# A graph layer on one core: each node search reads its own stretch of the loaded destinations, the load comes in two transfers, and the order test moves ahead of the first lists

## The chip, the cores and the metric

The kernel runs on one core of one Trainium2 chip. The metric is the device time of one execution in microseconds. Before the change it is 862.87 us, the median of 3 runs (862.81 to 863.2). The engines are TensorE (PE in the profile), VectorE (DVE), ScalarE (ACT), GpSimd (POOL) and SyncE (SP). SP, ACT and POOL issue transfers, and only POOL issues the indirect ones, which fetch from an address per partition.

## The reference

```python
def reference(x, src, dst, L0_gnn_W, L0_gnn_b):
    # x: 6250 nodes x 128; src, dst: 206250 edges, sorted by dst
    # (two random ends of 100000 edges, both ways, and one self edge per node)
    def _L0_gnn_ref(x, W, b, edge_index):
        src, dst = (edge_index[0], edge_index[1])
        x_i = x[dst]
        x_j = x[src]
        feat = jnp.concatenate([x_i, x_j - x_i], axis=-1)
        msg = feat @ W.T + b
        out = jax.ops.segment_max(msg, dst, num_segments=x.shape[0])
        return jnp.where(jnp.isfinite(out), out, 0.0)
    edge_index = jnp.stack([src, dst])
    h = jnp.maximum(_layernorm(x, axis=-1), 0.0)
    x = x + _L0_gnn_ref(h, L0_gnn_W, L0_gnn_b, edge_index)
    return x
```

Per node it is a maximum, over the node's incoming edges, of a row computed from the source node ("near"), plus a part of the node's own.

## The kernel before

**Tiling.** The 6250 nodes lie as 128 partitions by 49 columns; partition p owns nodes 49p to 49p+48. The edges are sorted by destination, so a partition's edges are one stretch of `dst` and `src`.

**Finding the edges (L925 to L976).** 512 samples of `dst`, one each `hop` = 403 edges, are compared with each partition's first node; a product on PE counts them (`count_ps`), and DVE turns the count into `begin_i`, the edge at which the partition's window begins. POOL then issues one indirect transfer (L713): every partition loads WIN = 2196 destinations. DVE casts them to f32 (L986), and `find` (L960) looks for the partition's 49 nodes and the next one, eight nodes per instruction, seven instructions, each over all 2196 columns. `find(0, 16)` and `begins(0)` give the start and the length of the list of the first 15 columns, the rest of `find` and `begins(1)` those of the other 34. Between them stand `statistics` and `scales`, which normalise x. When the starts are known, POOL issues one indirect transfer per column (L719, 15 and then 34), which loads the sources of 64 edges for each node.

**Lists (L1025), sort, words, compaction.** For each of the two parts (columns 0 to 14, columns 15 to 48) DVE masks the lists, sorts them by a network of 21 steps and packs those edges which the dense part below can't serve ("losers") into a list of 136, then 368, entries per partition.

**Two ways to the maximum.** Losers go through the chain: POOL gathers one row of `near_table` per partition and entry (L746, 503 gathers), and DVE takes a running maximum (`chain_step`, L1278). All others go through 196 dense rounds: ACT makes a one-hot matrix, PE multiplies (L869), DVE takes the maximum (L1334). At the end 49 final gathers on POOL (L725) fetch each node's chain result, and DVE joins both.

**What sets the order.** `schedule()` writes DVE's order after the first list by hand: a row of pieces with assumed costs (lists, three pieces named "check", 21 sorts, flags, words, moves, dense rounds, trees), between which it puts groups of 4 chain steps as soon as its assumed clock says that their rows have landed. The three "check" pieces are the order test: are the destinations sorted, and does every node occur? They read all of `dst` a second time, loaded by SP as `chk_i` (L434), 125 partitions by 1650, and write flags that are summed later. `then` and `settled` are a count of DVE's own finished instructions and a wait for it.

Queues: SP issues the samples, six chunks of x (L429; the fourth waits for `begin_ready`), the last rows of x, then waits for the window (`win_in`) and issues `chk_i` and x once more by rows. POOL issues the window, then waits for `starts_ready`.

Of the kernel before, what the change touches and what calls it, by code (L numbers as in the profile page):

```python
# [13 lines left out]
P = 128  # L14
F32 = mybir.dt.float32
# [19 lines left out]
SPAN = 1792  # L35

# [65 lines left out]
def schedule():  # L102
# [4 lines left out]
    pieces = [("lists", 11.0, 2.2), ("check", 1.1, 1.5), ("check", 1.9, 1.5), ("check", 1.9, 1.5)]  # L107
# [50 lines left out]
def edgeconv(nc, x, src, dst, W, b, out):  # L158
# [38 lines left out]
    with ExitStack() as ctx:  # L197
        def sb(name, shape, dt):
            return ctx.enter_context(nc.sbuf_tensor(name, shape, dt))

        def sem(name):
            return ctx.enter_context(nc.semaphore(name))
# [51 lines left out]
        begin_i = sb("begin_i", [P, 1], I32)  # L254
        pos = sb("pos", [P, 56], U32)
# [8 lines left out]
        flags = sb("flags", [P, 11], F32)  # L264
        flag_s = sb("flag_s", [P, 11], F32)
# [41 lines left out]
        def bank(i):  # L307
            return ps[:, i * 512:(i + 1) * 512]
# [7 lines left out]
        flag_ps = bank(7)[:, 0:11]  # L316
# [22 lines left out]
        win_in = sem("win_in")  # L339
# [82 lines left out]
        def _(sp):  # L422
            with nc.allow_non_contiguous_dma(reason="one edge in every hop"):
                smp_src = bass.AP(dst.tensor, dst.offset, [[4 * hop, P], [hop, 4]])
                sp.dma_start(smp_i[:, :], smp_src).then_inc(smp_in, 16)
            for c, (a, z) in enumerate(chunks):
                if c == 3:
                    sp.wait_ge(begin_ready, 1)
                sp.dma_start(x_nat[:, a:z, :], x_tiles[:, a:z, :]).then_inc(x_in[c], 16)  # L429
            sp.wait_ge(x_pad_set, 1)  # L430
            sp.dma_start(x_nat[0:rest, full, :], x[full * P:nodes, :]).then_inc(x_in[len(chunks)], 16)
            sp.wait_ge(win_in, 16)
# [263 lines left out]
        def _(pool):  # L696
# [5 lines left out]
            nc.gpsimd.memset(x_nat[:, full, :], 0.0).then_inc(x_pad_set, 1)  # L702
            nc.gpsimd.iota(iot_s, [[1, KS * 15]], base=1, channel_multiplier=0).then_inc(iota_set, 1)
# [3 lines left out]
            for q in range(1, len(opens)):  # L707
                if opens[q] > opens[q - 1]:
# [4 lines left out]
            nc.gpsimd.indirect_dma_start(win_i, None, dst[:, None],  # L713
                                         bass.IndirectOffsetOnAxis(begin_i[:, 0:1], 0)).then_inc(win_in, 16)
# [171 lines left out]
        def _(dve):  # L886
            own = [0]

            def then(ins):
                own[0] += 1  # L890
                ins.then_inc(dve_step, 1)

            def settled():
                dve.wait_ge(dve_step, own[0])
# [65 lines left out]
            def find(a, z):  # L960
                for c in range(a, z, 8):
                    then(V.max_index(pos[:, c:c + 8], tgt[:, c:c + 8], win))

            def begins(h):
# [3 lines left out]
                then(V.tensor_copy(start[:, at], pos[:, at]))  # L968
# [16 lines left out]
            dve.wait_ge(win_in, 16)  # L985
            then(V.tensor_copy(win, win_i))  # L986
# [3 lines left out]
            statistics(1)  # L990
            find(16, 32)
# [5 lines left out]
            then(V.tensor_tensor(flags[:, 0:1], win[:, WIN - 1:WIN], tgt[:, tiles:wide], ALU.is_lt))  # L997
            settled()
# [7 lines left out]
            def check():  # L1006

                dve.wait_ge(chk_in, 32)
                then(V.tensor_copy(chk[0:chk_p, :], chk_i[0:chk_p, :]))
                yield  # L1010
# [4 lines left out]
                yield  # L1015
# [3 lines left out]
                yield  # L1019
# [315 lines left out]

            lists(0)
# [9 lines left out]
            checks, flagging, wording, moving = check(), loser_flags(1), second_words(), compact(1)  # L1346
# [70 lines left out]
```

## Time and profile before

| | |
|---|---|
| median of 3 runs | 862.87 us |
| profiled execution, first to last instruction (the page gives no other time of it) | 862.0 us |
| DVE busy | 790.4 us, 92% |
| POOL busy | 619.0 us, 72% |
| PE busy | 544.8 us, 63% |
| ACT busy | 422.6 us, 49% |
| gathers L746 on POOL | 503, 516.1 us, mean 1026 ns |
| dense maxima L1334 on DVE | 196, 343.5 us |
| chain steps L1278 on DVE | 503, 176.8 us |

Busy time of POOL leaves out the 0.30 us that it takes between two gathers without waiting for anything; the profile puts it down as "issue". So a POOL that issues without a break looks 76% busy. Times below are from the start of the span.

### The profile page before, as it was taken

To read this page: it belongs to the slowest core of one execution; us is meant where nothing else is said; L and a number is where in the kernel's file an instruction comes from. 1 tells how busy PE (TensorE), PEld (TensorE's weight loads), DVE (VectorE), ACT (ScalarE), POOL (GpSimd) and SP (SyncE) were. 2 spreads that over 40 slices of the span, in tenths; PEclk is the share of its full clock that TensorE was granted. 3 is DMA by queue.
4 is the path that set the end of the run, shared out by engine and by line. 5 is a ranking of instruction groups with operands and counts; after the bars stand their busy time and mean duration, and the time that the engine had idled before them with its cause. 6 is when DMAs were issued, how large, how long until landed. Compare 5 with 4: busy or idle time off the path is not lost.

```text
span 862.0 us, 8032 instructions
## 1 busy us (share of the span) xinstructions
PE 544.8 (63%) x2442; PEld 263.8 (31%) x2442; DVE 790.4 (92%) x1283; ACT 422.6 (49%) x279; POOL 619.0 (72%) x631
## 2 busy tenths in 40 slices
PE   1565898000000677787766857788888888888871
PEld 1553466000000223232222323233333333333341
DVE  7989999989999899989989899899999998898897
ACT  3785314060147077656577569655565655742000
POOL 1577267788777777677777776777767777777774
PEclk9799899555555799988989988999999999999995
DMA  8951003232374766455655556556555666444347
GB/s 253 218 153 25 10 15 95 69 83 68 96 210 99 237 165 197 134 176 141 184 155 169 155 139 184 157 182 191 173 174 177 193 180 221 159 118 138 76 96 212
DMA packets 114693, 126.74 MB, mean 147 GB/s; under 512 B 19542, under 2 KB 96836, under 8 KB 114379
## 3 DMA queue, kind: packets, MB, share of 16 engines
q1 hardware_dynamic: 95090, 86.33, 33.0%
q0 software_dynamic: 19376, 38.94, 18.2%
q10 hardware_dynamic: 184, 0.96, 0.3%
q8 instruction: 19, 0.31, 0.1%
q14 instruction: 24, 0.20, 0.1%
HBM read 86.43 MB, written 40.57 MB: 147 GB/s over the span
## 4 chain that ended last, share of the span: by engine, by line
DVE 41%; POOL 19%; issue 19%; DMA 11%; PE 7%; ACT 1%; POOLq 0%; DVEq 0%; SPq 0%
POOL rows L746 14%; DMA rows<-near_table,idx 8%; DVE maxima L1278 8%; DVE acc L1334 8%; PE ps L869 7%; POOL hT L725 3%; DVE ohs L1240 3%; DVE sorts_mem L1068 2%; DVE sorts_mem L1067 2%; DVE hT L1287 2%; DVE ohs L1231 2%; POOL ohs L719 2%; DVE ohs L1229 1%; DVE rows L1240 1%; DMA ohs<-in_dst,begin_i 1%
## 5 line engine op out<-in xcount | busy, mean ns | idle before, releaser
L746 POOL DMA_INDIRECT rows<-near_table,idx x503 | 516.1, 1026 | 181.2 <-issue 132.8
L869 PE MATMUL ps<-ohs,near 128*128 128x481 fp8e3 x1404 | 319.0, 381 | 82.9 <-DVE acc L1334 76.3
L1334 DVE TENSOR_TENSOR acc<-ps,acc 128x1924 f32<-128x1924 f32 x196 | 343.5, 1779 | 29.3 <-PE ps L869 29.0
L607 ACT ACTIVATE ohs<-ohs,spike 128x6272 fp8e3<-128x6272 uint8 x36 | 197.9, 5513 | 72.0 <-DMA ohs<-winners 72.0
L869 PEld LDWEIGHTS ps<-ohs,near 128*128 128x128 bf16 x1404 | 134.3, 100 | 267.7 <-DVE acc L1334 90.2
L1278 DVE SCALAR_TENSOR_TENSOR maxima<-maxima,fresh,rows 128x128 f32<-128x128 f32 x503 | 176.8, 351 | 17.3 <-DMA rows<-near_table,idx 3.6
L602 ACT ACTIVATE hT<-k,off 128x1600 bf16<-128x1600 int16 (+6 forms) x49 | 65.9, 1392 | 154.8 <-DVE hT L1292 154.8
L869 PE MATMUL ps<-sorts_mem,near 128*128 128x481 fp8e3 x507 | 116.3, 385 | 28.1 <-DVE acc L1334 25.4
L607 ACT ACTIVATE sorts_mem<-sorts_mem,spike 128x6272 fp8e3<-128x6272 uint8 x13 | 71.7, 5515 | 35.9 <-DMA sorts_mem<-winners 35.9
L857 PE MATMUL ps<-flags,ones 128*128 128x11 f32 x2 | 0.6, 362 | 138.5 <-DVE spare L1312 138.5
L869 PEld LDWEIGHTS ps<-sorts_mem,near 128*128 128x128 bf16 x507 | 49.2, 101 | 94.9 <-DVE acc L1334 31.0
L719 POOL DMA_INDIRECT ohs<-src_pad,start_i x49 | 52.2, 1066 | 31.2 <-DVE start_i L975 16.9
L725 POOL DMA_INDIRECT hT<-running_max,end_row x49 | 47.0, 959 | 14.9 <-issue 14.3
L857 PEld LDWEIGHTS ps<-flags,ones 128*128 128x128 f32 x2 | 0.5, 310 | 138.6 <-issue 138.6
L589 ACT COPY base<-ps 128x512 f32<-128x512 f32 (+1 forms) x13 | 7.3, 562 | 40.7 <-PE ps L840 40.7
L1240 DVE COPY_PREDICATED ohs<-ohs 128x556 int32<-128x556 int32 (+9 forms) x40 | 26.2, 730 | 0.1
L840 PEld LDWEIGHTS ps<-wT,hT 128*128 128x128 f32 x98 | 23.5, 309 | 5.1 <-issue 3.7
L785 PE MATMUL ps<-ident,k 128*128 128x128 f32 x49 | 10.0, 335 | 23.3 <-ACT k L544 23.3
L811 PE MATMUL ps<-wT,hT 128*128 128x128 f32 x98 | 13.9, 285 | 15.8 <-ACT near L574 15.8
L840 PE MATMUL ps<-wT,hT 128*128 128x128 f32 x98 | 22.3, 373 | 0.0
L544 ACT ACTIVATE k<-acc,shift,rstd 128x128 f32<-128x128 f32 x49 | 20.1, 482 | 2.7 <-DVE shift L957 2.7
L614 ACT ACTIVATE ohs<-sorts_mem,j_bias 128x64 int32<-128x64 int16 x34 | 10.4, 403 | 22.2 <-DVE k L1075 22.2
(192 smaller groups left out, 472.6 us busy)
## 6 DMA issues: line engine op xcount, KB each, us to landing
running_max<-maxima SPq DMA_DIRECT2D x63, 512.0 KB, 3.6
ohs<-winners SPq DMA_DIRECT2D x36, 784.0 KB, 6.1
sorts_mem<-winners SPq DMA_DIRECT2D x13, 784.0 KB, 6.2
rows<-near_table,idx POOLq DMA_INDIRECT x503, 3.1
acc<-in_x SPq DMA_DIRECT2D x6, 512.0 KB, 8.0
near_table<-acc SPq DMA_DIRECT2D x12, 256.0 KB
base<-in_x SPq DMA_DIRECT2D x1, 2744.0 KB
out_x<-hT SPq DMA_DIRECT2D x12, 224.0 KB
```

The source lines that it names most:

```text
L544: last = nc.scalar.activation(xn[:, g % 2, j - spans[g][0], :], x_nat[:, j, :], ACT.Identity, bias=shift[:, j:j + 1], scale=rstd[:, j:j + 1])
L602: nc.scalar.activation(y[g % 2][:, t - a, 0:end - first, :], k2[:, first:end, :], ACT.Abs, bias=off[:, t:t + 1]).then_inc(y_made, 1)
L607: nc.scalar.activation(oh[t % OHS], oh_bytes[t % OHS], ACT.Abs_reciprocal_sqrt, bias=spike[:, 0:1], scale=float(SPIKE), saturate=False).th ...
L719: nc.gpsimd.indirect_dma_start(L[:, j, :], None, src_pad[:, None], bass.IndirectOffsetOnAxis(start_i[:, j:j + 1], 0)).then_inc(list_in[h], 16)
L725: nc.gpsimd.indirect_dma_start(rowsF[:, j, :], None, running_max[0:cap * P, :], bass.IndirectOffsetOnAxis(end_row[:, j:j + 1], 0)).then_in ...
L746: nc.gpsimd.indirect_dma_start(rows[:, n % (SLOTS * GATHERS), :], None, near_table[:, :], bass.IndirectOffsetOnAxis(idx[:, n:n + 1], 0)).t ...
L840: last = nc.tensor.matmul(bank(g % 3)[:, (j - a) * D:(j - a + 1) * D], hT[:, j:j + (P - 1) * tiles + 1:tiles], wT[:, 1, :], start=False, s ...
L869: last = nc.tensor.matmul(bank(4 * (n % 2) + c - UNITS[r][0])[:, 0:CHUNK], near[:, t, part, :], oh[t % OHS][:, at:at + CHUNK], start=part ...
L1067: then(V.tensor_tensor(two[:, :, 0:d, :], one[:, :, 0:d, :], one[:, :, d:2 * d, :], ALU.min))
L1240: then(V.copy_predicated(two[:, u:v], off_word[:, u + d:v + d], one[:, u:v]))
L1278: V.scalar_tensor_tensor(run_at(n + 1), run_at(n), fresh[:, n:n + 1], rows[:, n % (SLOTS * GATHERS), :], ALU.add, ALU.max).then_inc(chain, 1)
L1334: V.tensor_tensor(into, found[:, 0:z - a, 0:CHUNK], into, ALU.max).then_inc(max_done, 1)
```

## The change

- Partition 127's window is no longer computed: SP loads the last 1093 destinations into it right after the samples. The other 127 partitions load their window in two indirect transfers, columns 0 to 1026 (`win_in[0]`) and 1027 to 2195 (`win_in[1]`). The rest of partition 127's row is filled by a memset. `begin_i` is written straight from a clamp with per-partition bounds.
- `find` looks for the eight nodes of group k only in columns 236k-76 to 735+292k, cut to the window: 735, 867, 923, 979, 1035, 1091 and 856 columns, instead of seven times 2196. `look_i`, made on POOL, is added to the positions. Three new flags test that the stretches were wide enough.
- Two searches stand behind the cast of the near part; the far part is cast after `statistics(1)`.
- On SP the fourth chunk of x waits for the near part, and `chk_i` for the far part.
- The order test runs ahead of `lists(0)` in one piece; "check" is gone from the table, which changes where chain steps stand: 100 instead of 104 are done ahead of the sum of the flags, and 16 instead of 12 (504 places in all) are left behind the dense rounds.

```diff
 SPAN = 1792
+LAST_SPAN = 1093
+FAR_NODE = 1 << 16
+LOOK_FROM, LOOK_FROM_STEP = -76, 236
+LOOK_TO, LOOK_TO_STEP = 735, 292
+NEAR_SPAN = LOOK_TO + LOOK_TO_STEP
...
-    pieces = [("lists", 11.0, 2.2), ("check", 1.1, 1.5), ("check", 1.9, 1.5), ("check", 1.9, 1.5)]
+    pieces = [("lists", 11.0, 2.2)]
...
                 sp.dma_start(smp_i[:, :], smp_src).then_inc(smp_in, 16)
+            sp.dma_start(win_i[P - 1:P, 0:LAST_SPAN], dst[edges - LAST_SPAN:edges][None, :]).then_inc(last_in, 16)
             for c, (a, z) in enumerate(chunks):
                 if c == 3:
-                    sp.wait_ge(begin_ready, 1)
+                    sp.wait_ge(win_in[0], 16)
...
-            sp.wait_ge(win_in, 16)
+            sp.wait_ge(win_in[1], 16)
...
             nc.gpsimd.memset(x_nat[:, full, :], 0.0).then_inc(x_pad_set, 1)
+            nc.gpsimd.iota(look_i[:, :, :], [[LOOK_FROM_STEP, 7], [0, 8]], base=LOOK_FROM, channel_multiplier=0)
+            pool.drain()
+            nc.gpsimd.memset(look_i[:, 0, :], 0).then_inc(look_set, 1)
...
-            nc.gpsimd.indirect_dma_start(win_i, None, dst[:, None],
-                                         bass.IndirectOffsetOnAxis(begin_i[:, 0:1], 0)).then_inc(win_in, 16)
+            nc.gpsimd.indirect_dma_start(win_i[0:P - 1, 0:NEAR_SPAN], None, dst[:, None],
+                                         bass.IndirectOffsetOnAxis(begin_i[0:P - 1, 0:1], 0)).then_inc(win_in[0], 16)
+            pool.wait_ge(far_ready, 1)
+            nc.gpsimd.indirect_dma_start(win_i[0:P - 1, NEAR_SPAN:WIN], None, dst[:, None],
+                                         bass.IndirectOffsetOnAxis(far_i[0:P - 1, 0:1], 0)).then_inc(win_in[1], 16)
...
+            then(V.tensor_scalar(is_last[:, :], part_f[:, :], float(P - 1), None, ALU.is_equal))
...
+            then(V.tensor_scalar(begin_min[:, :], is_last[:, :], float(edges - LAST_SPAN), None, ALU.mult))
+            then(V.tensor_scalar(begin_max[:, :], is_last[:, :], float(WIN - LAST_SPAN), float(edges - WIN), ALU.mult, ALU.add))
+            then(V.memset(win_i[96:P, LAST_SPAN:WIN], FAR_NODE))
             dve.wait_ge(count_made, 1)
...
-            then(V.tensor_scalar(begin_f[:, :], begin_f[:, :], 0.0, float(edges - WIN), ALU.max, ALU.min))
+            V.tensor_scalar(begin_i[:, :], begin_f[:, :], begin_min[:, 0:1], begin_max[:, 0:1], ALU.max, ALU.min).then_inc(begin_ready, 1)
+            then(V.tensor_scalar(begin_f[:, :], begin_f[:, :], begin_min[:, 0:1], begin_max[:, 0:1], ALU.max, ALU.min))
             settled()
-            V.tensor_copy(begin_i[:, :], begin_f[:, :]).then_inc(begin_ready, 1)
+            V.tensor_scalar(far_i[:, :], begin_f[:, :], float(NEAR_SPAN), None, ALU.add).then_inc(far_ready, 1)
...
             def find(a, z):
-                for c in range(a, z, 8):
-                    then(V.max_index(pos[:, c:c + 8], tgt[:, c:c + 8], win))
+                for k in range(a // 8, z // 8):
+                    look = win[:, max(0, LOOK_FROM + k * LOOK_FROM_STEP):min(LOOK_TO + k * LOOK_TO_STEP, WIN)]
+                    then(V.max_index(pos[:, 8 * k:8 * k + 8], tgt[:, 8 * k:8 * k + 8], look))
...
-                then(V.tensor_copy(start[:, at], pos[:, at]))
+                then(V.tensor_tensor(start[:, at], pos[:, at], look_i[:, :, :].rearrange("p g n -> p (g n)")[:, at], ALU.add))
...
-            dve.wait_ge(win_in, 16)
-            then(V.tensor_copy(win, win_i))
+            dve.wait_ge(look_set, 1)
+            dve.wait_ge(last_in, 16)
+            dve.wait_ge(win_in[0], 16)
+            then(V.tensor_copy(win[:, 0:NEAR_SPAN], win_i[:, 0:NEAR_SPAN]))
             settled()
             find(0, 16)
             begins(0)
             statistics(1)
+            dve.wait_ge(win_in[1], 16)
+            then(V.tensor_copy(win[:, NEAR_SPAN:WIN], win_i[:, NEAR_SPAN:WIN]))
+            settled()
             find(16, 32)
...
+            then(V.scalar_tensor_tensor(flags[:, 11:12], win[:, 0:1], tgt[:, 0:1], is_last[:, :], ALU.is_ge, ALU.mult))
+            then(V.tensor_tensor(looked[:, :], tgt[:, 8:56:8], past[:, 8:56:8], ALU.add))
...
+            then(V.scalar_tensor_tensor(looked[:, :], starts_at, 0.0, looked[:, :], ALU.add, ALU.is_ge, accum_out=flags[:, 12:13]))
+            settled()
+            then(V.scalar_tensor_tensor(looked[:, :], win[:, LOOK_TO - 1:LOOK_TO + 5 * LOOK_TO_STEP:LOOK_TO_STEP], 0.0,
+                                        tgt[:, 7:48:8], ALU.add, ALU.is_lt, accum_out=flags[:, 13:14]))
...
+            check()
             lists(0)
...
-                if name == "check":
-                    next(checks)
```

The order of DVE's instructions changes in three places that the prediction speaks of. The first is around the window (`ohs`), from its cast to the first starts. Before:

```order
L984 CAST iot<-rows 128x960
L986 CAST ohs<-ohs 128x2196
L962 MAX_INDEX pos<-tgt,ohs 128x8 x2
L968 CAST start<-pos 128x16
L970 SCALAR_TENSOR_TENSOR start<-start,begin_f,past 128x16
L972 TENSOR_SCALAR start<-start 128x16
L975 CAST start_i<-start 128x15
```

After:

```order
L1011 CAST iot<-rows 128x960
L1015 CAST ohs<-ohs 128x1027
L989 MAX_INDEX pos<-tgt,ohs 128x8 x2
L995 TENSOR_TENSOR start<-pos,look_i 128x16
L997 SCALAR_TENSOR_TENSOR start<-start,begin_f,past 128x16
L999 TENSOR_SCALAR start<-start 128x16
L1002 CAST start_i<-start 128x15
```

The cast covers fewer columns, and the far part's cast (L1021, 128x1169) now stands behind `statistics(1)`. The second place is the end of the searches and the start of the first lists (`sorts_mem`). Before:

```order
L997 TENSOR_TENSOR flags<-ohs,tgt 128x1
L999 TENSOR_REDUCE spare<-deg 128x1
L1001 TENSOR_SCALAR flags<-spare 128x1
L1002 MEMSET maxima 128x128
L1003 TENSOR_SCALAR j_bias<-iota_f 128x49
L1028 TENSOR_TENSOR sorts_mem<-iota_f,deg 128x64x15
```

After:

```order
L1034 SCALAR_TENSOR_TENSOR looked,flags<-ohs,looked 128x6
L1036 SCALAR_TENSOR_TENSOR looked,flags<-ohs,tgt 128x6
L1039 TENSOR_REDUCE spare<-deg 128x1
L1041 TENSOR_SCALAR flags<-spare 128x1
L1042 MEMSET maxima 128x128
L1043 TENSOR_SCALAR j_bias<-iota_f 128x49
L1048 CAST ohs<-ohs 125x1651
L1051 SCALAR_TENSOR_TENSOR ohs,flags<-ohs 125x1650
L1054 SCALAR_TENSOR_TENSOR ohs,flags<-ohs 125x1650
L1064 TENSOR_TENSOR sorts_mem<-iota_f,deg 128x64x15
```

The order test, three long instructions, stands ahead of the first list's first instruction. The third place is where it stood, between the second lists and their sort; L1278 (L1314 after) are chain steps. Before:

```order
L1036 SCALAR_TENSOR_TENSOR sorts_mem<-sorts_mem 128x64x34
L1009 CAST ohs<-ohs 125x1651
L1013 SCALAR_TENSOR_TENSOR ohs,flags<-ohs 125x1650
L1017 SCALAR_TENSOR_TENSOR ohs,flags<-ohs 125x1650
L1278 SCALAR_TENSOR_TENSOR maxima<-maxima,fresh,rows 128x128 x4
L1067 TENSOR_TENSOR sorts_mem<-sorts_mem 128x32x35
L1068 TENSOR_TENSOR sorts_mem<-sorts_mem 128x32x35
```

After:

```order
L1072 SCALAR_TENSOR_TENSOR sorts_mem<-sorts_mem 128x64x34
L1103 TENSOR_TENSOR sorts_mem<-sorts_mem 128x32x35
L1104 TENSOR_TENSOR sorts_mem<-sorts_mem 128x32x35
L1097 TENSOR_TENSOR sorts_mem<-sorts_mem 128x16x2x35
L1098 TENSOR_TENSOR sorts_mem<-sorts_mem 128x16x2x35
L1103 TENSOR_TENSOR sorts_mem<-sorts_mem 128x32x35
L1104 TENSOR_TENSOR sorts_mem<-sorts_mem 128x32x35
L1314 SCALAR_TENSOR_TENSOR maxima<-maxima,fresh,rows 128x128 x4
```

Three steps of the sort (two instructions each) now stand ahead of the first four chain steps, where the order test stood.

## Rows read from the trace of the kernel before

**Rows 1.** The page: span, and busy time of each engine.
```profile
span 862.0 us, 8032 instructions
PE 544.8 (63%) x2442; PEld 263.8 (31%) x2442; DVE 790.4 (92%) x1283; ACT 422.6 (49%) x279; POOL 619.0 (72%) x631
```
**Rows 2.** Chain of waits, 0 to 125 us: start, length, what.
```profile
9.42 9.42 DMA ohs<-in_dst,begin_i
...
44.30 4.90 DMA ohs<-src_pad,start_i
```
**Rows 3.** DVE's timeline, 0 to 60 us: start, length, line, shape, [idle before].
```profile
1.57 2.40 DVE L897 MEMSET base<- 32x2816 f32 x1 [1.57 <-PEq L1408]
...
8.60 0.16 DVE L928 TENSOR_SCALAR begin_f<-ps 128x1 f32<-128x1 f32 x1 [1.51 <-PE ps L773]
...
16.04 0.65 DVE L984 CAST iot<-rows 128x960 int16<-128x960 int32 x1
18.87 1.30 DVE L986 CAST ohs<-ohs 128x2196 f32<-128x2196 int32 x1 [2.18 <-DMA ohs<-in_dst,begin_i]
20.21 0.09 DVE L962 MATCH_VALUE_LOAD pos<-tgt,ohs 128x8 f32 x1
...
22.64 0.07 DVE L962 MATCH_VALUE_LOAD pos<-tgt,ohs 128x8 f32 x1
...
25.86 0.17 DVE L975 CAST start_i<-start 128x15 int32<-128x15 f32 x1
...
49.30 1.16 DVE L1028 TENSOR_TENSOR sorts_mem<-iota_f,deg 128x960 int16<-128x960 f32 x1 [2.97 <-DMA ohs<-src_pad,start_i]
```
**Rows 4.** POOL's timeline, the same columns.
```profile
26.81 0.95 POOL L719 DMA_INDIRECT ohs<-src_pad,start_i  x1 [16.28 <-DVE start_i L975]
...
49.57 1.71 POOL L719 DMA_INDIRECT ohs<-src_pad,start_i  x1 [0.30 <-issue]
...
113.45 3.17 POOL L746 DMA_INDIRECT rows<-near_table,idx  x1 [19.49 <-DVE idx L1259]
...
125.12 2.31 POOL L746 DMA_INDIRECT rows<-near_table,idx  x1 [0.30 <-issue]
127.73 1.61 POOL L746 DMA_INDIRECT rows<-near_table,idx  x1 [0.30 <-issue]
```
**Rows 5.** DVE's timeline at the order test.
```profile
123.67 1.02 DVE L1009 CAST ohs<-ohs 125x1651 f32<-125x1651 int32 x1
124.73 1.88 DVE L1013 SCALAR_TENSOR_TENSOR ohs<-ohs 125x1650 f32<-125x1650 f32 x1
...
126.65 1.88 DVE L1017 SCALAR_TENSOR_TENSOR ohs<-ohs 125x1650 f32<-125x1650 f32 x1
...
128.45 1.52 DVE L1278 SCALAR_TENSOR_TENSOR maxima<-maxima,fresh,rows 128x128 f32<-128x128 f32 x4
```
**Rows 6.** Waits of POOL from 113 us on: us in total, times, longest.
```profile
POOL rows L746 <- DVE maxima L1278: 15.2, 36, 1.6
...
POOL rows L746 <- DMA rows<-near_table,idx: 13.7, 31, 2.7
```
**Rows 7.** POOL's timeline: its last gather.
```profile
852.22 1.02 POOL L725 DMA_INDIRECT hT<-running_max,end_row  x1 [0.30 <-issue]
```
**Rows 8.** DVE's timeline: its last wait.
```profile
856.56 0.29 DVE L1391 TENSOR_TENSOR hT<-ps,hT 128x128 f32<-128x128 f32 x1 [0.16 <-DMA hT<-running_max,end_row]
```
**Rows 9.** Transfers: count, and median us from issue to landing.
```profile
ohs<-src_pad,start_i POOLq DMA_INDIRECT x49, 2.9
```
**Rows 10.** Windows: busy of PE, PEld, DVE, ACT, POOL; clock, DMA share, GB/s.
```profile
8.00:10.00 2.00, 1.17 (x5) 0.77 (x5) 1.33 (x8) 0.00 (x0) 0.58 (x1) 1.00 0.42 126
10.00:12.00 2.00, 0.08 (x1) 0.00 (x0) 2.00 (x12) 1.66 (x2) 0.53 (x1) 1.00 0.99 283
...
50.00:113.00 63.00, 43.72 (x213) 29.09 (x214) 60.85 (x140) 33.18 (x60) 34.81 (x31) 0.95 0.20 45
```
**Rows 11.** The page: the costliest group of POOL.
```profile
L746 POOL DMA_INDIRECT rows<-near_table,idx x503 | 516.1, 1026 | 181.2 <-issue 132.8
```

More of the change, by code:

```diff
@@ L254, in edgeconv @@
         begin_i = sb("begin_i", [P, 1], I32)
+        far_i = sb("far_i", [P, 1], I32)
+        begin_min = sb("begin_min", [P, 1], F32)
+        begin_max = sb("begin_max", [P, 1], F32)
+        is_last = sb("is_last", [P, 1], F32)
+        look_i = sb("look_i", [P, 7, 8], I32)
+        looked = sb("looked", [P, 6], F32)
         pos = sb("pos", [P, 56], U32)
@@ L263, in edgeconv @@
         end_row = sb("end_row", [P, tiles], I32)
-        flags = sb("flags", [P, 11], F32)
-        flag_s = sb("flag_s", [P, 11], F32)
+        flags = sb("flags", [P, 14], F32)
+        flag_s = sb("flag_s", [P, 14], F32)
         disorder = sb("disorder", [P, 1], I32)
@@ L315, in edgeconv @@
         count_ps = bank(7)[:, 256:257]
-        flag_ps = bank(7)[:, 0:11]
+        flag_ps = bank(7)[:, 0:14]
         x_pad_set = sem("x_pad_set")
@@ L338, in edgeconv @@
         begin_ready = sem("begin_ready")
-        win_in = sem("win_in")
+        win_in = [sem(f"win_in{i}") for i in range(2)]
+        last_in = sem("last_in")
+        far_ready = sem("far_ready")
+        look_set = sem("look_set")
         starts_ready = sem("starts_ready")
@@ L997, in _ @@
             then(V.tensor_tensor(flags[:, 0:1], win[:, WIN - 1:WIN], tgt[:, tiles:wide], ALU.is_lt))
+            then(V.scalar_tensor_tensor(flags[:, 11:12], win[:, 0:1], tgt[:, 0:1], is_last[:, :], ALU.is_ge, ALU.mult))
+            then(V.tensor_tensor(looked[:, :], tgt[:, 8:56:8], past[:, 8:56:8], ALU.add))
+            settled()
+            starts_at = win[:, LOOK_FROM + LOOK_FROM_STEP:LOOK_FROM + 6 * LOOK_FROM_STEP + 1:LOOK_FROM_STEP]
+            then(V.scalar_tensor_tensor(looked[:, :], starts_at, 0.0, looked[:, :], ALU.add, ALU.is_ge, accum_out=flags[:, 12:13]))
+            settled()
+            then(V.scalar_tensor_tensor(looked[:, :], win[:, LOOK_TO - 1:LOOK_TO + 5 * LOOK_TO_STEP:LOOK_TO_STEP], 0.0,
+                                        tgt[:, 7:48:8], ALU.add, ALU.is_lt, accum_out=flags[:, 13:14]))
             settled()
@@ L1009, in check @@
                 then(V.tensor_copy(chk[0:chk_p, :], chk_i[0:chk_p, :]))
-                yield
                 settled()
@@ L1014, in check @@
                                             ALU.add, ALU.is_lt, accum_out=flags[0:chk_p, 2:3]))
-                yield
                 settled()
@@ L1018, in check @@
                                             ALU.add, ALU.not_equal, accum_out=flags[0:chk_p, 3:4]))
-                yield
             def columns(h):
@@ L1344, in _ @@
             loser_list(0)
-            checks, flagging, wording, moving = check(), loser_flags(1), second_words(), compact(1)
+            flagging, wording, moving = loser_flags(1), second_words(), compact(1)
             wordings, sorts, trees_begun, left_of_tree, dense_rounds = 0, 0, 0, 0, 0
```

## The prediction

> **What bounds the kernel now.** I read the page first [rows 1, 11]: DVE is busy 92% of 862.0 us and POOL 72%, but POOL also spends 0.30 us ahead of nearly every gather with nothing to wait for, so 72% hides how full its queue is. Next the waits of POOL from 113 us on [rows 6]: 36 waits for chain steps and 31 for landed rows, 28.9 us in all; 0.30 us of each is the usual gap, so 28.9 - 67 x 0.30 = 8.8 us is real waiting. That is enough to add up POOL's stream. Its first row gather starts at 113.45 [rows 4], its last final gather at 852.22 [rows 7], 738.8 us apart. In between go 503 + 49 = 552 gathers; at 0.95 + 0.30 us each [rows 4] they take 690 us. The 503 average 1026 ns instead of 950 [rows 11], which is 38 us of stretching, and with the 8.8 us of waits the sum is 737 us. So from the moment when the first loser list is ready, POOL issues almost without a break to the end. DVE ends with it: its last wait is 0.16 us, for the last final gather [rows 8]. Two full queues end together, and a gain must move both.
>
> What starts POOL's stream is DVE's first list (`idx`), and DVE sits on the path to it: its lists, sort and packing fill 49.30 to 113.45 (60.85 us busy of the 63 from 50 to 113 [rows 10], the rest being gaps of a few hundredths behind each instruction). What it waited for at 49.30 are the 15 list gathers [rows 2, 3], which hang on the first starts at 26.03, and these on the window: issued 9.42, landed 18.84 [rows 2]. The search section is therefore on the path up to the first starts, and not behind them: DVE sat idle for 2.97 us there although it had done the other five searches.
>
> **The first starts.** Removed: the wait of 2.18 us, and part of the cast (1.30 us for 2196 columns, so 0.61 to 0.66 us for 1027) [rows 3], 0.65 us. A search takes 22.64 - 20.21 = 2.43 us for 2196 columns, 0.07 us of it the load of the eight values [rows 3]. By columns 735 cost 0.86 us and 867 cost 1.00 us; two searches go from 4.86 to 1.86 us, a gain of 3.0 us. (If nothing scaled, the gain would be 0; a scan over columns leaves no reason for that.) Added ahead of `begin_i`: a memset of 1103 columns, 0.94 us by 2.40 us for 2816, and four one-column operations of at most 0.15 us, 1.5 us by the full lengths; DVE idles there for 1.51 us [rows 3], so it is covered, just. `begin_i` comes 0.2 us sooner, as a step is cut. Behind it a clamp and `far_i` put `statistics(0)` back by about 0.2 us. Sum: 2.18 + 0.65 + 3.0 - 0.2 = 5.6 us earlier, first starts at 20.4, first list gather at 21.2 instead of 26.81 [rows 4].
>
> That holds if the near part lands by 16.9, where DVE is ready for it. The whole window took 9.42 us with three chunks of x beside it [rows 2]; now those chunks wait, the near part has 47% of the bytes, and just before the issue the DMA engines were only 0.42 busy [rows 10]. 0.47 x 9.42 = 4.4 us gives 13.8. If it took 9.42 us again, it would land at 18.7 and cost 1.8 us; I keep that as a bound and take none. The late chunks are wanted by `statistics(1)` at 20.4: issued around 14, 1.6 MB and 0.6 MB of far part at 283 GB/s [rows 10] take 8 us, to 22, while its last chunk is read at 23.6. No wait, at worst 1 to 2 us, in front of a wait of DVE that is longer.
>
> **The order test ahead of the first lists.** DVE used 20.3 us from the starts at 26.03 to 46.33, which is 49.30 less the idle 2.97 [rows 3]. Five searches of 4884 columns in all go from 12.15 to 5.6 us. Added: the far part's cast 0.70 us, four small flag operations 0.7 us (five, with their waits, bounded by 0.15 and 0.30 us each), and the order test, 128.53 - 123.67 = 4.85 us [rows 5]. 20.3 - 6.55 + 0.7 + 0.7 + 4.85 = 20.0 us: done at 40.4. The list gathers, unhindered, would land at 49.2 - 5.6 = 43.6. So DVE's own time is hidden, with 3.2 us to spare; without that cover the test would cost its 4.85 us here.
>
> But POOL is not unhindered. A gather that starts while DVE runs an instruction with two inputs from SBUF does not end before it: 49.57 lasts 1.71 us while L1028 runs until 50.46; 125.12 and 127.73 last 2.31 and 1.61 us, and end 0.8 to 0.9 us behind the two comparisons of the order test [rows 3 to 5]. In the new place the cast runs from 35.6, the comparisons from 36.6 to 38.5 and from 38.5 to 40.4. The last three of the 15 gathers are due at 36.2, 37.4 and 38.7. The first of them waits for the cast's end and is over at 37.4; the next starts at 37.7, waits until 38.5 and is over at 39.35; the last starts at 39.65, waits until 40.4 and is over at 41.25 instead of 39.65. Cost 1.6 us; from 0 (if all comes later than reckoned here) to 2.8 us (if a third gather is caught). So the first lists start 5.6 - 1.6 = 4.0 us earlier. The landing took 4.90 us from the last issue [rows 2], the median is 2.9 us [rows 9]: up to 2 us more gain, unclaimed.
>
> The Trainium skill (SBUF — State Buffer, "Who interferes with whom") infers that an operation with two SBUF inputs holds only the read side of the port that DVE and GpSimd share, and so does not hold up descriptor generation. By that rule the comparisons would cost POOL nothing in either place, and the change would be worth the 5.6 us alone, 857.3 us. The trace speaks against it, with the 2.31 and 1.61 us above.
>
> **The order test gone from its old place.** DVE is freed of 4.85 us behind 123.67, and with four chain steps fewer ahead of the flags' sum (1.5 us by 1.52 for four [rows 5]) the dense rounds begin up to 6.3 us sooner on top. POOL gets only what the two comparisons had cost it: 2.31 + 1.61 - 2 x 0.95 = 2.0 us. The bounds are 0 (POOL runs into its limit of 24 rows ahead of the chain, since the chain steps themselves come only about 1 us sooner: three sorts now stand ahead of them) and 4.85 us (if POOL follows DVE). I take 2.0, as POOL's real waits are only 8.8 us over the run. At the end DVE has steps enough in hand: 16 instead of 12 behind the rounds add 1.5 us there. What is late next is POOL's last gather, and DVE will wait for it.
>
> The second part's 34 list gathers left POOL by 113.45 - 19.49 = 93.96 [rows 4], while `lists(1)` begins with the first loser list done; they stay hidden. `far_i`'s wait on POOL has nothing queued behind it that is due before the starts.
>
> **Sum.** 4.0 + 2.0 = 6.0 us. The profiled execution spans 862.0 us and the median run is 862.87; the 0.9 us around the span stays. 862.87 - 6.0 = 856.9 us. What a measurement can tell from no change is 0.2%, 1.7 us.
>
> **Rivals.**
> - *Only part of it arrives.* The list gathers are caught three times (2.8 us), and POOL, nearer to its limit, gives the 2.0 us back as waits for chain steps: 5.6 - 2.8 = 2.8 us, 860.1 us. For it: 36 releases by chain steps, the longest wait 1.6 us [rows 6]. Against: only 4.4 us of these are real waiting. 20%.
> - *DVE is the bound, not POOL.* Then all that DVE is freed of counts: 5.6 + 4.85 = 10.4 us, 852.5 us. For it: DVE at 92%, and any stretch in which its work stops POOL's. Against: the sum of POOL's stream, and rows 8. 15%.
> - *Slower: the reload of `dst` is late.* The order test is now first in DVE's queue ahead of all lists, and its data are issued only when the far part has landed. DVE would wait at L1048 with the first lists behind it. If the data land at time t, the lists start at t + 4.85; this eats the gain of 4.0 us at t = 44.45 and the whole of it, old place included, at 46.45; from 48.2 the kernel is measurably slower. At t = 50 it is 862.87 + 3.6 = 866.4 us. For it: 3.1 MB of x by rows are issued right behind. Against: they are behind, not ahead; 0.83 MB at 283 GB/s [rows 10] take 3 us from about 20. 5%.
> - *The change does little.* A new table of chain steps that makes DVE wait for rows which its clock takes for landed, or a near part at 18.7 together with the first rival: 2.8 - 1.8 = 1.0 us, 861.9 us. 5%.
>
> The forecast has 55%, with a range of its own of 854.6 to 859.2 (landing 2 us shorter, or gathers caught once more). With the rivals of 860.1 and 852.5 taken in until two in ten are left out, the range is 853.3 to 860.8. Faster 0.91 (55 + 20 + 15, and a share of the last), same 0.04, slower 0.05.
>
> **What would show it.** The window's wait of 2.18 us gone and the first list gather near 21.2; searches of 0.86 to 1.3 us; two or three of the last 15 list gathers stretched to 1.5 us and more; a wait of DVE of 3 to 5 us ahead of the first lists, at about 45.3; the first row gather at about 109.5; its neighbours at 125 no longer stretched by comparisons; at the end a wait of DVE for final gathers of some us instead of 0.16. I am wrong if DVE waits for x in `statistics(1)` or for `dst` at the order test, or if POOL's real waits grow beyond 8.8 us by as much as the list came earlier.

## The result and the profile after

The changed kernel takes 883.55 us (median of 4 runs, 880.72 to 884.89), the kernel before 863.04 us beside it. The ratio is 1.023 with a 95% interval of 1.0211 to 1.0249: slower by 2.3%, where 856.9 us and faster was forecast. The profiled execution took 880.72 us, its span is 879.1 us, 17.1 us longer than before [rows 1]. It was the fastest of the four, so the trace accounts for 17.1 of the 20.5 us between the medians.

The timeline of DVE in the changed kernel (start, length, line, shape, idle time before and who ended it), at the places of [rows 3]:

```profile
7.55 0.98 DVE L951 MEMSET ohs<- 32x1103 int32 x1 [0.28 <-issue]
8.61 0.16 DVE L953 TENSOR_SCALAR begin_f<-ps 128x1 f32<-128x1 f32 x1
...
16.34 0.66 DVE L1011 CAST iot<-rows 128x960 int16<-128x960 int32 x1
34.92 0.70 DVE L1015 CAST ohs<-ohs 128x1027 f32<-128x1027 int32 x1 [17.92 <-DMA ohs<-in_dst,begin_i]
35.65 0.09 DVE L989 MATCH_VALUE_LOAD pos<-tgt,ohs 128x8 f32 x1
35.73 0.92 DVE L989 FIND_INDEX8 pos<-tgt,ohs 128x8 uint32<-128x735 f32 x1
...
38.39 0.17 DVE L1002 CAST start_i<-start 128x15 int32<-128x15 f32 x1
...
44.44 5.15 DVE L966 BATCH_NORM_STATS2 ohs<-acc 128x6 f32<-128x128 f32 x25 [5.80 <-DMA acc<-in_x]
...
65.09 1.02 DVE L1048 CAST ohs<-ohs 125x1651 f32<-125x1651 int32 x1 [5.02 <-DMA ohs<-in_dst]
...
72.51 1.16 DVE L1064 TENSOR_TENSOR sorts_mem<-iota_f,deg 128x960 int16<-128x960 f32 x1 [2.55 <-DMA ohs<-src_pad,start_i]
```

DVE is ready for the near part at 17.0 and waits 17.92 us for it. The first search takes 0.92 us for 735 columns, close to the 0.86 forecast. Then DVE waits for x (5.80 us), for `dst` (5.02 us) and for the list gathers. The chain of waits from 0 to 70 us (start, length, what) has two transfers where [rows 2] has them:

```profile
9.39 25.40 DMA ohs<-in_dst,begin_i
...
57.28 15.20 DMA ohs<-src_pad,start_i
```

Between them lies the whole delay of the first lists, 72.51 - 49.30 = 23.2 us: the first starts come 38.56 - 26.03 = 12.5 us later, the landing of the 15th list gather takes 15.20 - 4.90 = 10.3 us longer, 0.4 us is issue. SP issued the second load of x only at 46.3, instead of 19.6, since it stands behind the far part; e6 shows what such a load does to a landing. POOL's timeline, the same columns, beside [rows 4] and [rows 7]:

```profile
9.39 2.84 POOL L731 DMA_INDIRECT ohs<-in_dst,begin_i  x1 [5.62 <-DVE begin_i L955]
12.53 2.55 POOL L734 DMA_INDIRECT ohs<-in_dst,far_i  x1 [0.31 <-issue]
...
136.55 3.17 POOL L767 DMA_INDIRECT rows<-near_table,idx  x1 [29.22 <-DVE idx L1295]
...
869.34 0.94 POOL L746 DMA_INDIRECT hT<-running_max,end_row  x1 [0.30 <-issue]
```

POOL's stream, by which I mean the time from its first row gather to its last final gather, begins 23.1 us later and lasts 732.8 us instead of 738.8; so it ends 17.1 us later, as the span does. DVE now waits for it at the end, 3.86 us instead of 0.16 [rows 8]:

```profile
872.09 0.69 DVE L1426 TENSOR_TENSOR hT<-ps,hT 128x512 f32<-128x512 f32 x1 [3.86 <-DMA hT<-running_max,end_row]
```

What is wrong with the two window transfers shows in the windows, whose last columns are granted clock, DMA share and GB/s:

```profile
10.00:20.00 10.00, 1.47 (x6) 0.71 (x4) 6.45 (x33) 4.58 (x10) 4.78 (x2) 1.00 0.31 45
20.00:36.00 16.00, 8.34 (x48) 7.48 (x48) 1.05 (x3) 9.56 (x23) 0.00 (x0) 1.00 0.13 48
```

Before, the same stretches moved 303 and 217 GB/s. Now, from 20 to 36 us, the share of 0.13 of 16 engines, which is two, moves 48 GB/s, while SP's further loads wait for the two parts. The page's row on the software queue (packets, MB, share) counts more packets as well: before it had 19376 for nearly the same bytes.

```profile
q0 software_dynamic: 23328, 38.95, 18.2%
```

### The profile page after: what moved, and what is told of

It is laid out like the page before. It is cut to its first block, busy times and chain, and to the rows that moved or that the text cites. A ratio compares the mean times of both kernels' runs of the same rounds, so it can differ in the third digit from the quotient of the medians.

```text
span 879.1 us, 8050 instructions
## 1 busy us (share of the span) xinstructions
PE 541.9 (62%) x2442; PEld 263.6 (30%) x2442; DVE 783.1 (89%) x1295; ACT 422.4 (48%) x279; POOL 621.0 (71%) x634
## 4 chain that ended last, share of the span: by engine, by line
DVE 56%; issue 17%; PE 13%; POOL 6%; DMA 5%; ACT 0%; DVEq 0%; POOLq 0%
DVE acc L1370 19%; PE ps L890 13%; DVE maxima L1314 13%; DMA ohs<-in_dst,begin_i 3%; POOL rows L767 3%; DVE ohs L1276 3%; DVE hT L1323 2%; POOL hT L746 2%; DVE sorts_mem L1104 2%; DVE sorts_mem L1103 2%; DMA ohs<-src_pad,start_i 2%; POOL ohs L740 2%; DVE ohs L1267 2%; DVE ohs L1265 1%; DVE rows L1276 1%
## 5 line engine op out<-in xcount | busy, mean ns | idle before, releaser
L890 PE MATMUL ps<-ohs,near 128*128 128x481 fp8e3 x1404 | 315.2, 378 | 79.6 <-DVE acc L1370 73.4
L1314 DVE SCALAR_TENSOR_TENSOR maxima<-maxima,fresh,rows 128x128 f32<-128x128 f32 x503 | 176.9, 352 | 13.5
L890 PE MATMUL ps<-sorts_mem,near 128*128 128x481 fp8e3 x507 | 118.8, 390 | 29.0 <-DVE acc L1370 26.6
L890 PEld LDWEIGHTS ps<-sorts_mem,near 128*128 128x128 bf16 x507 | 49.3, 102 | 98.2 <-DVE acc L1370 33.7
L1323 DVE TENSOR_TENSOR hT<-hT 128x1600 bf16<-128x1600 bf16 (+7 forms) x25 | 20.7, 828 | 0.0
```

What stands on the lines that cost most here:

```text
L890: last = nc.tensor.matmul(bank(4 * (n % 2) + c - UNITS[r][0])[:, 0:CHUNK], near[:, t, part, :], oh[t % OHS][:, at:at + CHUNK], start=part ...
L1314: V.scalar_tensor_tensor(run_at(n + 1), run_at(n), fresh[:, n:n + 1], rows[:, n % (SLOTS * GATHERS), :], ALU.add, ALU.max).then_inc(chain, 1)
L1323: then(V.tensor_tensor(mine[:, 0:n, 0:half, :], mine[:, 0:n, 0:half, :], mine[:, 0:n, half:2 * half, :], ALU.min))
```

## The experiments

Theory A, made after the result: an indirect transfer over 127 partitions is spread over only about two of the 16 DMA engines. Rival B: splitting the window in two, or holding x back, is the cause.

**e1: the kernel before, its one window transfer over 127 partitions.**

```diff
+            sp.dma_start(win_i[P - 1:P, :], dst[edges - WIN:edges][None, :]).then_inc(last_in, 16)
...
-            nc.gpsimd.indirect_dma_start(win_i, None, dst[:, None],
-                                         bass.IndirectOffsetOnAxis(begin_i[:, 0:1], 0)).then_inc(win_in, 16)
+            nc.gpsimd.indirect_dma_start(win_i[0:P - 1, :], None, dst[:, None],
+                                         bass.IndirectOffsetOnAxis(begin_i[0:P - 1, 0:1], 0)).then_inc(win_in, 16)
...
+            dve.wait_ge(last_in, 16)
```

> The kernel before with one edit: the window's one indirect transfer covers 127 partitions instead of 128, and partition 127's 2196 destinations come by a plain transfer of SP (its window begins at edges - 2196 there anyway). Theory A (an indirect transfer over 127 partitions is spread over about 2 of the 16 DMA engines, since the DMA share in the changed kernel was 0.13 from 20 to 36 us at about 50 GB/s): the window of 1.12 MB lands about 22 us after it begins to move, near 33 us instead of 18.8, and the kernel is slower than before by 14 to 20 us, 877 to 883 us; the DMA share falls to about 0.13 while it is under way. Theory B (it is the split into two transfers, or x being held back until the near part is in): no change, 863 us, window still in 9.4 us.

903.61 us, ratio 1.0479 (1.0462 to 1.0497): 41 us slower from one partition fewer. The window landed 51.8 us after its issue instead of 9.4. Its windows, the same columns as above:

```profile
20.00:36.00 16.00, 8.50 (x48) 7.64 (x48) 0.00 (x0) 10.45 (x24) 0.00 (x0) 1.00 0.06 26
```

0.06 of 16 engines is one engine, at 26 GB/s. The expectation said two engines and 877 to 883 us, since it took the two transfers of the changed kernel for one; the near and the far part went through one engine each. B, which forecast no change, is out as the cause of this; e2 keeps the split and the held x, and e5 has no plain transfer beside the indirect one.

**e2: the changed kernel, both parts over 128 partitions.**

```diff
-LAST_SPAN = 1093
+LAST_SPAN = 1027
...
-            sp.dma_start(win_i[P - 1:P, 0:LAST_SPAN], dst[edges - LAST_SPAN:edges][None, :]).then_inc(last_in, 16)
...
-            nc.gpsimd.indirect_dma_start(win_i[0:P - 1, 0:NEAR_SPAN], None, dst[:, None],
+            nc.gpsimd.indirect_dma_start(win_i[:, 0:NEAR_SPAN], None, dst[:, None],
...
-            nc.gpsimd.indirect_dma_start(win_i[0:P - 1, NEAR_SPAN:WIN], None, dst[:, None],
+            nc.gpsimd.indirect_dma_start(win_i[:, NEAR_SPAN:WIN], None, dst[:, None],
...
-            then(V.memset(win_i[96:P, LAST_SPAN:WIN], FAR_NODE))
+            then(V.tensor_scalar(last_far[:, :], is_last[:, :], float(FAR_NODE), None, ALU.mult))
...
-            then(V.tensor_copy(win[:, NEAR_SPAN:WIN], win_i[:, NEAR_SPAN:WIN]))
+            then(V.tensor_scalar(win[:, NEAR_SPAN:WIN], win_i[:, NEAR_SPAN:WIN], last_far[:, 0:1], None, ALU.max))
```

> The changed kernel with both parts of the window loaded over all 128 partitions; partition 127 begins at edges - 1027, so its near part is exact, and its far part is overwritten on DVE by a maximum with a large number in the far part's cast (instead of the memset). Theory A (127 partitions are the fault): the near part lands by 14 to 16 us, DVE does not wait for it, and the prediction's own sum holds: 855 to 859 us. Theory B (two transfers, or x held back): near part still at 30 us and more, 878 us and more. If x issued behind the near part is late as well, statistics(1) waits 1 to 3 us, covered by the wait for the list gathers.

859.51 us, ratio 0.9961 (0.9947 to 0.9975): 24 us less than the change, a little faster than before, and just above the 855 to 859 expected. The software queue is back at 19520 packets. The near part took 5.2 us, DVE did not wait for it, and the first starts came at 20.6, forecast 20.4. Yet the first lists did not move. DVE's timeline, from the cast of the near part on:

```profile
16.96 0.69 DVE L1013 CAST ohs<-ohs 128x1027 f32<-128x1027 int32 x1
...
20.42 0.17 DVE L1001 CAST start_i<-start 128x15 int32<-128x15 f32 x1
...
32.24 0.32 DVE L980 RECIPROCAL rstd<-std 128x25 f32<-128x25 f32 x1 [2.71 <-ACT std L551]
...
41.95 1.88 DVE L1052 SCALAR_TENSOR_TENSOR ohs<-ohs 125x1650 f32<-125x1650 f32 x1
...
49.64 1.16 DVE L1062 TENSOR_TENSOR sorts_mem<-iota_f,deg 128x960 int16<-128x960 f32 x1 [5.80 <-DMA ohs<-src_pad,start_i]
```

The last of the 15 list gathers was issued at 38.86 and landed 10.75 us later. The gain of 5.4 us at the first starts ended in this wait of 5.80 us. POOL's first row gather starts at 113.64, 0.2 us later than before; what e2 gains is in the stream, which lasts 734.7 us instead of 738.8.

**e3: the kernel before, only the order test moved.** Its three instructions stand ahead of `lists(0)`, its pieces are out of the table.

```diff
-    pieces = [("lists", 11.0, 2.2), ("check", 1.1, 1.5), ("check", 1.9, 1.5), ("check", 1.9, 1.5)]
+    pieces = [("lists", 11.0, 2.2)]
...
+            for _ in check():
+                pass
             lists(0)
```

> The kernel before with only the order test moved ahead of the first lists (and its pieces gone from the table). DVE's searches are not shortened here, so the test's 4.85 us come on top of the path to the first lists less the 2.97 us of idle time: first lists 1.9 us later. If POOL sets the end: 1.9 us lost there, 2.0 us back from the two stretched gathers in the old place, and the last list gathers are not caught at all as they are issued before 45.2: 862 to 864 us. If DVE sets the end: 1.9 lost, 4.85 won, 859.5 to 860.5 us.

861.64 us, ratio 0.9986 (0.9972 to 0.9999): within what can be told from no change, and between the two forecasts (862 to 864 if POOL sets the end, 859.5 to 860.5 if DVE does), so the time alone decides nothing. In the trace DVE waits 4.71 us at the end for a final gather, as it should if POOL sets the end. The profiled execution, 865.57 us, was the slowest of ten. Its window landed 11.17 us after its issue instead of 9.42, which explains 1.75 of the 3.8 us by which its stream begins later. The stream runs from 117.22 to 853.97, 736.8 us against 738.8 before: the 2.0 us forecast for the old place, which the other kernels show to be the least that it is worth.

**e4: e2 with the order test in its old place.**

```diff
-            check()
             lists(0)
...
+                if name == "check":
+                    next(checks)
```

> e2 with the order test back in its old place (and its pieces back in the table): split, short searches, 128 partitions. First lists 5.6 us earlier than before, nothing else: 857 to 858 us if POOL sets the end. Against e2: by my sum e2 gains 2.0 us from the old place and loses 1.6 us by stretched list gathers, so e2 is 0 to 1 us faster; if DVE set the end, e2 would be 4 to 5 us faster.

862.06 us, ratio 0.9999 (0.9985 to 1.0012), where 857 to 858 was expected. Split and short searches alone were worth nothing. e2 is 2.5 us faster, between the 0 to 1 us expected if POOL sets the end and the 4 to 5 us if DVE does. e4's stream lasts 738.0 us, 3.2 us more than e2's. DVE's timeline has the gain as idle time:

```profile
48.80 1.16 DVE L1065 TENSOR_TENSOR sorts_mem<-iota_f,deg 128x960 int16<-128x960 f32 x1 [10.31 <-DMA ohs<-src_pad,start_i]
```

The first lists start at 49.3, 49.6 and 48.8 in before, e2 and e4, though the gathers went out 5 us sooner in e2 and e4: something else holds the landing at that time. Theory C: the second load of x (6250 rows of 512 bytes, 3.2 MB, issued at 20) fills the engines ahead of them. Rival D: the gathers themselves are slow.

**e5: row counts.** Eight further indirect transfers, one after the other, at the end of the kernel before.

```diff
+            for i, r in enumerate((128, 127, 126, 124, 120, 112, 96, 64)):
+                nc.gpsimd.indirect_dma_start(spot[0:r, :], None, dst[:, None],
+                                             bass.IndirectOffsetOnAxis(begin_i[0:r, 0:1], 0)).then_inc(sweep_in, 16)
+                pool.wait_ge(sweep_in, 16 * (i + 1))
```

> The kernel before, with eight more indirect transfers at the very end, one after the other, when all else is done: 2196 destinations per partition into memory no longer used, over 128, 127, 126, 124, 120, 112, 96 and 64 partitions. Only the length of each matters. 128 should take 5 to 7 us; 127 took 52 us in e1, on one DMA engine (share 0.06 at 26 GB/s). Theory A1 (the rows are dealt to as many engines as the largest number up to 16 that divides their count): 126 on 14 engines, 124 on 4, 120 on 15, 112, 96 and 64 on 16: 124 takes 11 us or more, the others 5 to 7. Theory A2 (the largest power of two up to 16 that divides the count): 126 on 2 engines, 22 us; 124 on 4, 11 us; 120 on 8, 7 us. Theory A3 (any count that 16 doesn't divide goes on one engine): 126, 124 and 120 all take 40 us and more.

POOL's timeline of the one execution; each row is the issue of one count, and the time from row to row is what a transfer took:

```profile
859.96 0.94 POOL L771 DMA_INDIRECT near<-in_dst,begin_i  x1 [8.29 <-DMA out_x<-hT]
866.35 2.55 POOL L771 DMA_INDIRECT near<-in_dst,begin_i  x1 [5.45 <-DMA near<-in_dst,begin_i]
912.99 0.98 POOL L771 DMA_INDIRECT near<-in_dst,begin_i  x1 [44.09 <-DMA near<-in_dst,begin_i]
919.54 1.29 POOL L771 DMA_INDIRECT near<-in_dst,begin_i  x1 [5.57 <-DMA near<-in_dst,begin_i]
936.85 0.98 POOL L771 DMA_INDIRECT near<-in_dst,begin_i  x1 [16.01 <-DMA near<-in_dst,begin_i]
945.17 0.94 POOL L771 DMA_INDIRECT near<-in_dst,begin_i  x1 [7.34 <-DMA near<-in_dst,begin_i]
952.37 0.92 POOL L771 DMA_INDIRECT near<-in_dst,begin_i  x1 [6.26 <-DMA near<-in_dst,begin_i]
958.69 0.89 POOL L771 DMA_INDIRECT near<-in_dst,begin_i  x1 [5.40 <-DMA near<-in_dst,begin_i]
```

In order: 128 partitions 6.4 us, 127 46.6, 126 6.6, 124 17.3, 120 8.3, 112 7.2, 96 6.3 us. Windows within the transfers over 127, 126, 124 and 120:

```profile
880.00:910.00 30.00, 0.00 (x0) 0.00 (x0) 0.00 (x0) 0.00 (x0) 0.00 (x0) 0.50 0.06 27
916.00:917.00 1.00, 0.00 (x0) 0.00 (x0) 0.00 (x0) 0.00 (x0) 0.00 (x0) 0.50 0.84 351
926.00:928.00 2.00, 0.00 (x0) 0.00 (x0) 0.00 (x0) 0.00 (x0) 0.00 (x0) 0.50 0.25 75
940.00:941.00 1.00, 0.00 (x0) 0.00 (x0) 0.00 (x0) 0.00 (x0) 0.00 (x0) 0.50 0.90 202
```

Shares of 0.06, 0.84, 0.25 and 0.90 are 1, about 14, 4 and about 15 engines: A1, the largest number up to 16 that divides the count. A2 would have put 126 on two engines and A3 on one. The 8.3 us of 120 partitions are more than A1 gave (5 to 7), those of 112 slightly; the engines of 120 were busy at only 202 GB/s, and why is open. Per engine the four windows show 27, 25, 19 and 13 GB/s, so the number of engines alone does not give the time. The kernel before already avoids the number 127 elsewhere: it loads x by rows in three transfers, over 112, 15 and 1 partitions.

The Trainium skill states this rule (DMA: Bandwidth & Descriptors, "Why a DMA increments its semaphore by 16 and not by 1"): the largest number of engines up to 16 that divides the slowest dimension of both access patterns, with 127 partitions on one engine as its example. The trace agrees, with the shares above.

**e6: e2 with the second load of x behind the stores of near_table.** The three transfers into `base` move, with their wait, below this loop on SP:

```diff
-            sp.wait_ge(base_pad_set, 1)
-            sp.dma_start(base[0:most, :, :], x_rows[0:most, :, :]).then_inc(xs_in, 16)
...
                 sp.dma_start(near_tiles[:, a:z, :], x_nat[:, a:z, :]).then_inc(near_out, 16)
+            sp.wait_ge(base_pad_set, 1)
+            sp.dma_start(base[0:most, :, :], x_rows[0:most, :, :]).then_inc(xs_in, 16)
...
```

> e2 with the second load of x (3.1 MB by rows into base, which PE reads only from about 92 us) issued behind the stores of near_table instead of ahead of them. In e2 the first starts came 5.4 us earlier, and the first lists not at all: the last of the 15 list gathers was issued at 38.9 and landed 10.75 us later. Theory C (it stands in the DMA engines behind the x rows): the landing takes 3 to 5 us, the first lists start at 43 to 45 instead of 49.6, and the kernel takes 853 to 855 us. Theory D (the gathers themselves, or POOL's stretched gathers behind the order test, are slow): no change, 859 us.

855.5 us, ratio 0.9916 (0.9903 to 0.993), 0.5 us above the range of theory C and far from the 859 of D. Theory C holds: from 20 to 36 us the DMA share is 0.53 instead of 1.08 in e2, the last list gather lands 2.8 us after its issue, DVE starts the first lists straight behind the order test, without a wait, and POOL's stream begins 5.3 us sooner than before. First DVE, then POOL:

```profile
32.33 0.32 DVE L980 RECIPROCAL rstd<-std 128x25 f32<-128x25 f32 x1 [2.80 <-ACT std L551]
...
43.77 1.16 DVE L1062 TENSOR_TENSOR sorts_mem<-iota_f,deg 128x960 int16<-128x960 f32 x1
```

```profile
108.15 3.18 POOL L766 DMA_INDIRECT rows<-near_table,idx  x1 [18.33 <-DVE idx L1293]
...
843.91 1.02 POOL L745 DMA_INDIRECT hT<-running_max,end_row  x1 [0.30 <-issue]
```

**e7: the kernel before with the same edit.**

> The kernel before with the same edit as e6. There the landing took 4.90 us; by theory C it falls to about 3, the first lists start 1 to 2 us earlier (DVE is done with its own work at 46.3), and the kernel takes 861 to 862 us. By theory D 862.9 us.

861.14 us, ratio 0.9985 (0.9973 to 0.9997). The landing fell from 4.90 to 2.47 us and the first lists from 49.30 to 46.34. In the traces the stream begins and ends 2.8 us sooner; by the medians the gain is 1.5 us, less than what can be told from no change.

**e8: the changed kernel, x not held back.**

```diff
                 if c == 3:
-                    sp.wait_ge(win_in[0], 16)
+                    sp.wait_ge(begin_ready, 1)
```

> The changed kernel with one edit: the fourth chunk of x waits for begin_ready, as before the change, and not for the near part. If one DMA engine carries the near part whatever else runs (theory A), the near part still lands at 33 to 36 us and more; the wait of 5.8 us for x in statistics(1) goes, so the second starts come earlier, but the first list gathers do not: 878 to 884 us. If holding x back were the cause (theory B), the near part would still have had an empty machine, so it can only get later; a fall below 870 us would speak for B.

880.66 us, ratio 1.0212 (1.0195 to 1.023), as expected. Holding x back is not the cause. The chain shows that the near part needed even longer. x moved beside it; that they shared an engine is not shown:

```profile
9.38 29.09 DMA ohs<-in_dst,begin_i
```

**e9: e6 with the order test in its old place** (the edit of e4).

> e6 (128 partitions, second load of x behind the stores) with the order test back in its old place and in the table. In e6 the first lists start at 43.8 without a wait, straight behind the order test. Without the test there they start when the list gathers have landed, 38.9 + 2.5 to 3 = 41.5 to 42. If POOL's stream sets the end, that is 2 us sooner at the start of the stream and 2 to 2.7 us more in it (two row gathers stretched by the comparisons): 855 to 856 us, the same as e6. If DVE set the end it would be 2 us sooner and 4.85 later: 858 to 859.

854.69 us, ratio 0.99 (0.9883 to 0.9918), not to be told from e6. If DVE set the end it would have been 858 to 859. POOL's timeline:

```profile
105.80 3.16 POOL L766 DMA_INDIRECT rows<-near_table,idx  x1 [18.31 <-DVE idx L1296]
...
844.77 1.02 POOL L745 DMA_INDIRECT hT<-running_max,end_row  x1 [0.31 <-issue]
```

Its stream begins 2.35 us sooner than in e6 and lasts 739.0 us against 735.8: what the moved order test costs at the head, it gives back in the stream, with 0.9 us over that the medians don't show.

**e10: e6, ScalarE's second square root one group sooner.**

```diff
-                if g == halves[0][1] // GROUP - 1:
+                if g == halves[0][1] // GROUP - 2:
                     deviations(1)
```

> e6 with ScalarE's square root for the second half of the tiles put one group sooner in its queue. In e6 VectorE waits 2.80 us for it between the searches, and this wait is now on the path to the first lists, since these start without a wait behind the order test. Expected: the wait falls to 0.5 us or less, the order test runs 2.3 us sooner, and the first lists start when the gathers have landed, at 42 to 43: 0.8 to 1.8 us better than e6, 853.7 to 854.7 us. It would be no gain if the comparisons then catch the last list gathers: up to 2.8 us, which would show as gathers of 1.6 to 2.3 us among the first 15.

854.17 us, ratio 0.9897 (0.9879 to 0.9915), the best of all, by no more than the noise. That it lies in the expected range is luck, for what was to bring the gain did not happen: the square root's wait was gone, but the first lists stayed at 43.88, where 42 to 43 was expected. Now the order test catches list gathers, in POOL's timeline.

```profile
36.60 1.65 POOL L739 DMA_INDIRECT ohs<-src_pad,start_i  x1 [0.30 <-issue]
38.56 1.61 POOL L739 DMA_INDIRECT ohs<-src_pad,start_i  x1 [0.30 <-issue]
40.47 1.62 POOL L739 DMA_INDIRECT ohs<-src_pad,start_i  x1 [0.30 <-issue]
```

Three gathers of 0.94 us take 1.6 us. They end 0.8 us behind the order test's cast (over at 37.44) and its two comparisons (39.36 and 41.28). They are the last three of the 15, and the 2.0 us lost lie in the prediction's range of 0 to 2.8.

**e11: e6, x not held back** (the edit of e8).

> e6 with the fourth chunk of x waiting for begin_ready and not for the near part. With the near part on all engines it then shares them with three chunks of x: near part lands at 16 to 18 instead of about 14, DVE wants it at 17. Expected 855 to 856.5 us, the same as e6 or up to 1 us slower.

854.66 us, ratio 0.9901 (0.988 to 0.9922). DVE waited 0.28 us for the near part and started the first lists at 43.50. Holding x back brought nothing.

## Why the prediction was wrong

- **The step that failed** is the landing of the near part: "0.47 x 9.42 = 4.4 us gives 13.8", with 18.7 as the bound. It landed at 34.8, 25.4 us after its issue. Both numbers scale by bytes and assume that a transfer over 127 partitions moves like one over 128. e1 and e5 show one engine instead of 16 for it; e2, with 128, took 5.2 us. The row that the bound leant on could not hold it: it was a transfer over another number of partitions. The rule is in the Trainium skill, and I had not weighed it.
- **The 4.90 us of landing taken as fixed.** "The list gathers, unhindered, would land at 49.2 - 5.6 = 43.6." e2 and e4 show 49.6 and 48.7, and before 49.2, though the last gather was issued 5 us sooner in them. It looks as if the 3.2 MB of x were worked off at about that time whatever is issued when, which is not shown. Shown is that with them out of the way the landing takes 2.4 to 2.8 us (e6, e7, e9). This took the whole 4.0 us forecast for the first lists: in e2 they started 0.3 us later than before.
- **Unforeseen: a wait for ScalarE.** "Done at 40.4" left out that DVE would wait for the square root of the second half of x, 2.71 us in e2. There the order test ended at 43.8, and its cast and comparisons caught one of the 15 list gathers, for 0.3 us, instead of costing 1.6. With the square root sooner (e10) they caught three and cost 2.0.
- **Right: the first starts.** 20.4 was forecast, 20.6 measured in e2. The memset was covered. The two searches took 2.0 us instead of 1.86, and `begin_i` came less than 0.1 us sooner instead of 0.2.
- **Right in direction, too small: what the order test costs POOL.** 2.0 us back was forecast. The seven streams with the test moved last 732.8 us (changed kernel) to 736.8 (e3), 734.6 on average; the four with it in place 738.0 (e4) to 739.0 (e9), 738.7 on average, so about 4 us. Pair by pair it is 2.0 (e3 against before) and 3.2 us (e2 against e4, and e6 against e9). The 503 row gathers themselves take 511.4 to 514.1 us instead of 515.2 to 516.4; the rest is waits and gaps. Which instructions beyond the two comparisons held POOL up is open. That two-input comparisons leave POOL alone, as the inference of the Trainium skill cited in the prediction has it, is refuted again by e10's second and third gather.
- **Right: POOL's stream sets the end.** The changed kernel and e2 to e11 end as the stream does; DVE, freed of 4.85 us, waits 3.9 us (changed kernel) or 2.8 us (e6) for a final gather, and with the test in place 0.2 to 0.6 us (before, e4, e9).
- **The rivals.** The slower one was named with the right symptom, a transfer that lands late in front of DVE, at the wrong place: DVE did wait 5.02 us for `dst` at the order test, but only since this load waits for the far part; in e2 and e6 this wait is gone. Both waits that the prediction named as signs of being wrong, for x and for `dst`, came.
- **The sum** of 6.0 us needed both missing conditions, 128 partitions and x out of the way; the second is an edit that the change did not have. e6, which has both, gains 7.1 us by its medians (855.5 against 862.6), within the forecast's own range, with other terms than forecast: its stream begins 5.3 us sooner (forecast 4.0) and is 3.0 us shorter (forecast 2.0). e2 gains 3.1 us, all of it from the stream.

## What to carry to other kernels

Cutting an indirect transfer from 128 partitions to 127 to spare a special row cost 40 us for 1.1 MB (e1, e5): keep the partition count a number with a large divisor up to 16, and load the odd row with the rest and mend it afterwards. A transfer's time may be scaled by its bytes only while its partition count stays. When a step on the path to a gather gets shorter, look at what fills the DMA engines when the gather lands: a large load that nobody needs yet belongs behind it.

## What the runs showed of the hardware

- Indirect transfers of 8784 bytes per partition, with nothing else running, in one execution (e5): 6.4 us over 128 partitions, 46.6 over 127, 6.6 over 126, 17.3 over 124. One engine moved 26 to 27 GB/s (e1, e5).
- Issuing the 127-partition transfer also kept POOL busy for 2.55 us instead of 0.94 (e5), and raised the count of packets, by 1904 in e1.
- A small gather issued behind the 3.2 MB load of x took 4.9 (before), 9.4 (e4), 10.8 (e2) and 15.2 us (changed kernel) to land, and 2.4 to 2.8 us without it (e6, e7, e9).
- An indirect gather issued while DVE ran the cast or one of the comparisons of the order test ended 0.8 us behind it and took 1.6 us instead of 0.94 (e10).
